# Layer 1's end rebuilt: gathers that centre by themselves, the bonus added in PSUM, the last state product on VectorE, the channel mix by halves in the same section

## What is computed

```python
def step(s, rkvw):                       # s: 8x8 state of each of 32 heads
    r_t, k_t, v_t, w_t = rkvw
    a = k_t[:, :, :, None] * v_t[:, :, None, :]
    out = jnp.einsum('bhk,bhkd->bhd', r_t, u * a + s)
    return (a + w_t[:, :, :, None] * s, out)
_, outs = jax.lax.scan(step, s0, xs)
a4 = outs as (b, l, H, 8)                # per head: subtract the mean, divide by the deviation
m = jnp.mean(a4, axis=-1, keepdims=True)
var = jnp.mean((a4 - m) ** 2, axis=-1, keepdims=True)
att = ((a4 - m) * jax.lax.rsqrt(var + EPS)).reshape(b, l, E) * gn_w + gn_b
x = x + att * g @ Wo.T
xn2 = _ln(x, ln2_w, ln2_b)
sx2 = _token_shift(xn2, state[:, i0])    # row before minus row
xk = xn2 + sx2 * ffn_maa_k
xr = xn2 + sx2 * ffn_maa_r
rr = jax.nn.sigmoid(xr @ ffn_Wr.T)
kk = jnp.square(jax.nn.relu(xk @ ffn_Wk.T))
x = x + rr * (kk @ ffn_Wv.T)
```

## Time and profile before

| | |
|---|---|
| median of the runs | 1258.51 us |
| the profiled execution | 1257.39 us, span 1255.70 |
| mean granted clock of TensorE | 0.981 |
| PE, DVE, ACT, POOL busy | 91%, 65%, 51%, 54% |
| state loop, layer 1's end | about 816 to 880 us, 880 to 942 us |

### The profile page before, as it was taken

One profiled execution on the slowest core, in us unless ns is written; L12 is line 12 of the kernel. 1 busy time (PEld: TensorE's weight loads), 2 busy tenths in 40 slices (PEclk: granted clock), 3 DMA queues, 4 the chain that ended last, 5 costly groups with the idle time before them and its releaser, 6 DMA issues. The chain is left out here.

```text
span 1255.7 us, 20660 instructions
## 1 busy us (share of the span) xinstructions
PE 1142.1 (91%) x7388; PEld 889.8 (71%) x7388; DVE 822.2 (65%) x2013; ACT 642.1 (51%) x1428; POOL 683.9 (54%) x742
## 2 busy tenths in 40 slices
PE   5999999999999999999998967987578999999996
PEld 4788888887978788888887852443355676667674
DVE  6776666676656766667666545598557655666774
ACT  3655654566545555565566111510325655777764
POOL 3656664666645656556575312386005655566874
PEclk9999999999999999999999988999889999999999
DMA  6210220121102210221020200000001100000000
GB/s 213 67 44 26 68 67 16 53 68 62 56 18 67 68 44 25 68 68 51 18 68 17 84 17 0 1 1 0 1 0 61 35 2 1 2 1 2 10 10 18
DMA packets 35111, 47.06 MB, mean 37 GB/s; under 512 B 3865, under 2 KB 22082, under 8 KB 35010
## 3 DMA queue, kind: packets, MB, share of 16 engines
q1 hardware_dynamic: 34640, 44.83, 11.3%
q10 hardware_dynamic: 370, 0.91, 0.2%
HBM read 44.69 MB, written 1.05 MB: 36 GB/s over the span
## 5 line engine op out<-in xcount | busy, mean ns | idle before, releaser
L444 POOL TENSOR_TENSOR a_prob<-a_prob,a_inv_total 128x512 f32<-128x512 f32 x128 | 144.2, 1126 | 208.2 <-DVE a_inv_total L732 208.2
L1967 POOL TENSOR_TENSOR scores<-scores,neg_max 128x512 f32<-128x512 f32 x144 | 147.5, 1040 | 77.4 <-DVE neg_max L1835 77.2
L637 ACT ACTIVATE a_prob<-psum,a_neg_max 128x257 f32<-128x257 f32 x256 | 119.0, 472 | 94.3 <-DVE a_neg_max L729 93.4
L1758 ACT ACTIVATE prob_T<-psum 128x512 f32<-128x512 f32 x192 | 113.1, 600 | 35.5 <-PE psum L1679 34.1
L1679 PE MATMUL psum<-ident,scores 128*128 128x128 f32 x768 | 117.8, 279 | 1.5 <-POOL scores L1967 1.5
L1679 PEld LDWEIGHTS psum<-ident,scores 128*128 128x128 f32 x768 | 85.7, 141 | 36.8 <-issue 16.3
L736 DVE TENSOR_TENSOR a_probT_lo<-psum,a_probT_hi 128x512 fp32r<-128x512 f32 x128 | 88.0, 687 | 32.5 <-ACT a_probT_hi L641 32.0
L1835 DVE CUSTOM_DVE_ANT_0 scores<-psum,ctx_rows 128x256 f32<-128x256 f32 x256 | 93.5, 420 | 18.7 <-PE psum L1666 9.3
L566 PE MATMUL psum<-ident,a_prob 128*128 128x128 f32 x512 | 77.8, 274 | 24.0 <-DVE a_probT_lo L736 21.7
L566 PEld LDWEIGHTS psum<-ident,a_prob 128*128 128x128 f32 x512 | 60.0, 140 | 44.5 <-issue 20.9
L641 ACT ACTIVATE a_probT_hi<-psum 128x512 fp32r<-128x512 f32 x128 | 76.7, 599 | 22.2 <-PE psum L566 22.2
(11 more groups left out here) (347 smaller groups left out, 3340.7 us busy)
## 6 DMA issues: line engine op xcount, KB each, us to landing
wk_raw<-in_L_xattn_wk SPq DMA_DIRECT2D x16, 512.0 KB, 6.3
wq_raw<-in_L_xattn_wq SPq DMA_DIRECT2D x16, 512.0 KB, 5.6
wv_raw<-in_L_xattn_wv SPq DMA_DIRECT2D x16, 512.0 KB, 3.7
wo_raw<-in_L_xattn_wo SPq DMA_DIRECT2D x16, 512.0 KB, 3.9
ctx_rows<-in_ctx SPq DMA_DIRECT2D x3, 512.0 KB, 4.1
x_rows<-in_x SPq DMA_DIRECT2D x2, 512.0 KB, 9.7
ctx_rows<-in_mask_Bx1xSxS_ff SPq DMA_DIRECT2D x1, 1024.0 KB, 5.5
out_dram<-x_rows SPq DMA_DIRECT2D x4, 256.0 KB, 2.1
```

The lines of the kernel that those rows point to most:

```text
L444: pool.tensor_tensor(prob[:, m % 4, :, 0:S], prob[:, m % 4, :, 0:S], rtot[:, m % 4, :].unsqueeze(2).to_broadcast([P, 2, S]), ALU.mult)
L637: act.activation(prob[:, m % 4, q, 0:S + 1], s_bank(g)[:, q, 0:S + 1], ACT.Exp, bias=negm[:, m % 4, q:q + 1], accum_out=tot[:, m % 4, q:q ...
L1758: act.activation(pT[:, i % PT, :], t_bank(i), ACT.Exp, scale=1.0 if on_scalar(i) else -1.0).then_inc(exp_ok, 1)
L1967: pool.tensor_tensor(sc[:, i % SC, :, :], sc[:, i % SC, :, :], m[:, i % SC, :].unsqueeze(2).to_broadcast([P, 2, S]), ALU.subtract).then_in ...
```

## The change

The gather matrices hold -1/8 for every row of the head and 7/8 for the row itself, so that what they sum has the head's mean subtracted; they are now made on DVE. A matrix `centre` (identity less 1/8 over the head) adds the bonus to the same banks, one matmul for each piece. Mean, centring and the adds on DVE are gone. The second half of the last product z is made by DVE. PE's order at the end of the loop is another. The banks of the following steps are swapped (variances and Wo in 0 to 3, layer norm in 4 to 7). The layer norm runs its statistics and normalise for both halves behind the adds. The channel mix stands in the same section, reuses the section's buffers and takes the tokens by halves; the sigmoid's scaling is folded into its last two operations.

```diff
 # PE
+                def gather_outputs(g, cs):
+                    for c in cs:
+                        pe.wait_ge(z_ok, NC * g + c + 1)
+                        for n in (2 * c, 2 * c + 1):
+                            mm = pe.matmul(ps[:, 4 + n, :], gather[:, g, :], z[g % 2][:, c, half(n)], start=g == 0, stop=g == S1 - 1)
+                            if g == S1 - 1:
+                                mm.then_inc(g_full, 1)
...
+                def gather_bonus(n):
...
+                    pe.matmul(ps[:, 4 + n, :], centre[:, :], att[:, n // 2, half(n)], start=False, stop=False)
+
+                for e in range(2, S1):
+                    spread_values(e, 0)
+                    if e == S1 - 1:
+                        gather_outputs(e - LATE, range(NC))
+                    spread_values(e, 1)
...
+                    if e < S1 - 1:
+                        gather_outputs(e - LATE, range(NC))
+                    if e >= 5:
+                        gather_bonus(e - 5)
+                gather_bonus(3)
+                gather_outputs(S1 - 2, range(NC))
+                gather_outputs(S1 - 1, range(NC))
...
 # DVE
+                dve.scalar_tensor_tensor(centre[:, :], same[:, :], -1.0 / S1, chip.ident[:, :], ALU.mult, ALU.add).then_inc(centre_ok, 1)
                 for e in range(S1):
-                    dve.tensor_copy(gather[:, e, e:P:S1], same[:, e:P:S1]).then_inc(gather_ok, 1)
+                    dve.tensor_scalar(gather[:, e, :], same[:, :], -1.0 / S1, None, ALU.mult).then_inc(gather_low, 1)
+                for e in range(S1):
+                    dve.wait_ge(gather_low, e + 1)
+                    dve.tensor_scalar(gather[:, e, e:P:S1], same[:, e:P:S1], 1.0 - 1.0 / S1, None, ALU.mult).then_inc(gather_ok, 1)
...
+                        if (e, c) == LAST:
+
+                            dve.wait_ge(g_full, S1 - 2)
+                            dve.wait_ge(st_ok, S1 * NC)
+                            dve.wait_ge(z_ok, S1 * NC - 1)
+                            dve.tensor_tensor(z[e % 2][:, c, :], rT[:, c, :], flat(state[:, e % 2, c, :, :]), ALU.mult).then_inc(z_ok, 1)
...
-                for i, n in enumerate(SEQ):
-                    dve.wait_ge(g_full, S1 + i)
-                    dve.tensor_tensor(att[:, n // 2, half(n)], att[:, n // 2, half(n)], ps[:, 4 + n, :], ALU.add).then_inc(att_ok, 1)
-                    if i >= 2:
-                        centre(i - 2)
...
-                    ln.after_rows(dve, q)
+                    if q % 2:
+                        ln.statistics(dve, q // 2)
+                for h in range(2):
+                    ln.normalise(dve, h)
+                channel_mix_vector(dve)
 # ACT
+                for n in range(4):
+                    act.wait_ge(g_full, S1 + n)
+                    act.activation(sq[:, n // 2, half(n)], ps[:, 4 + n, :], ACT.Square).then_inc(sq_ok, 1)
 # the channel mix: DVE, then PE
+            for h in range(2):
+                dve.wait_ge(ln.turned_out, 2 * h + 2)
+                for c in range(NC):
+                    dve.tensor_tensor(sx2[:, c, two(h), :], xe[:, c, two(h), 0:S], xe[:, c, two(h), 1:R1], ALU.subtract).then_inc(cm_shifted, 1)
+                mix(xk, 'L1_xattn_ffn_maa_k', h)
+                mix(xr, 'L1_xattn_ffn_maa_r', h)
+                if h:
+                    for c in range(NC):
+                        square(c, 0)
+            for c in range(NC):
+                square(c, 1)
...
+            for h in range(2):
+
+                pe.wait_ge(cm_mixed, 4 * h + 2)
+                for c in range(NC):
+                    n = 2 * c + h
+                    for k in range(NC):
+                        mm = pe.matmul(ps[:, n, :], w['ffn_Wk'][:, k, c * P:(c + 1) * P], flat(xk[:, k, two(h), :]), start=k == 0, stop=k == NC - 1)
+                    mm.then_inc(k_full, 1)
+                pe.wait_ge(cm_mixed, 4 * h + 4)
+                pe.wait_ge(ln.turned_out, 4)
+                for t in range(4 * h, 4 * h + 4):
...
```

More of the change, by code:

```diff
@@ L928, in stage_rwkv @@
         kv_of = lambda c: ps[:, 2 * c:2 * c + 2, :].rearrange("p h n -> p (h n)")
+        cm_first, cm_shifted, cm_mixed, k_full, relu_ok, kk_ok, r_full, tanh_ok, o2_full, t_ok = (
+            chip.semaphore(f"cm_{n}") for n in ("first", "shifted", "mixed", "k_full", "relu_ok", "kk_ok", "r_full", "tanh_ok", "v_full", "t_ok"))
+        sx2, xr = wT, first
+        xk = rT[:, :, :].rearrange("p c (b s) -> p c b s", s=S)
+        kk = state[:, 0].rearrange("p c b s -> p c (b s)")
+        tanh_r = state[:, 1].rearrange("p c b s -> p (c b s)").rearrange("p (t n) -> p t n", n=D)
@@ new lines, in stage_rwkv, with channel_mix_vector, mix, square @@
+        gated_v = scaled[:, 0].rearrange("p c n -> p (c n)").rearrange("p (t n) -> p t n", n=D)
+        two = lambda q: slice(2 * q, 2 * q + 2)
+        def channel_mix_vector(dve):
+            def mix(dst, name, h):
+                for c in range(NC):
+                    dve.wait_ge(cm_shifted, 2 * h + c + 1)
+                    dve.scalar_tensor_tensor(dst[:, c, two(h), :], sx2[:, c, two(h), :], chip.vec(name, c), xe[:, c, two(h), 1:R1], ALU.mult, ALU.add).then_inc(cm_mixed, 1)
+            def square(c, h):
+                dve.wait_ge(relu_ok, 2 * h + c + 1)
+                n = 2 * c + h
+                dve.scalar_tensor_tensor(kk[:, c, half(n)], ps[:, n, :], 0.0, kk[:, c, half(n)], ALU.max, ALU.mult).then_inc(kk_ok, 1)
+            dve.wait_ge(cm_first, 1)
+            for h in range(2):
[9 more added lines that the diff above has]
+                square(c, 1)
+            for q in range(4):
+                dve.wait_ge(o2_full, q + 1)
+                dve.wait_ge(tanh_ok, q + 1)
+                dve.scalar_tensor_tensor(gated_v[:, two(q), :], tanh_r[:, two(q), :], 1.0, ps[:, 2 * (q % 2) + q // 2, :].rearrange("p (j n) -> p j n", j=2), ALU.add, ALU.mult).then_inc(t_ok, 1)
+                dve.wait_ge(t_ok, q + 1)
+                dve.scalar_tensor_tensor(chip.x[:, two(q), :], gated_v[:, two(q), :], 0.5, chip.x[:, two(q), :], ALU.mult, ALU.add)
@@ new lines, in channel_mix_scalar @@
+        def channel_mix_scalar(act):
+            for h in range(2):
+                for c in range(NC):
+                    n = 2 * c + h
+                    act.wait_ge(k_full, 2 * h + c + 1)
+                    act.activation(kk[:, c, half(n)], ps[:, n, :], ACT.Relu).then_inc(relu_ok, 1)
+                for q in (2 * h, 2 * h + 1):
+                    act.wait_ge(r_full, q + 1)
+                    act.activation(tanh_r[:, two(q), :], ps[:, 4 + q, :].rearrange("p (j n) -> p j n", j=2), ACT.Tanh, scale=0.5).then_inc(tanh_ok, 1)
@@ L1029, in _ @@
+                    if e >= 5:
[4 more added lines that the diff above has]
+                for n in range(4):
+                    pe.wait_ge(sq_ok, n + 1)
+                    pe.matmul(ps[:, n, :], same[:, :], sq[:, n // 2, half(n)], start=True, stop=True).then_inc(var_full, 1)
                 for t in range(NT):
                     if t % 4 == 0:
-                        pe.wait_ge(gated, 2 + 2 * (t // 4))
@@ L1098, in _, with norm @@
                             dve.scalar_tensor_tensor(gT[:, c, half(n)], tanh_of(n), 1.0, ps[:, bank_of(('pg', n)), :], ALU.add, ALU.mult).then_inc(dve_free, 1)
[L1100 removed]
+                def norm(i):
                     n = SEQ[i]
[L1102 to L1112 removed]
+                    dve.wait_ge(rstd_ok, i + 1)
+                    dve.scalar_tensor_tensor(att[:, n // 2, half(n)], ps[:, 4 + n, :], chip.vec('L1_xattn_gn_w', n // 2), sq[:, n // 2, half(n)], ALU.mult, ALU.mult).then_inc(gn_ok, 1)
                 def gate(i):
@@ L1118, in gate @@
                                              ALU.add, ALU.mult).then_inc(gated, 1)
-                for i, n in enumerate(SEQ):
-                    c = n // 2
-                    dve.wait_ge(rstd_ok, i + 1)
-                    dve.scalar_tensor_tensor(att[:, c, half(n)], att[:, c, half(n)], chip.vec('L1_xattn_gn_w', c), sq[:, c, half(n)], ALU.mult, ALU.mult).then_inc(gn_ok, 1)
+                for i in range(4):
+                    norm(i)
                     if i:
```

160 lines of the change are left out of this document (45 added, 115 removed).

## The result

The changed kernel takes 1246.26 us (median of 4 runs, 1244.27 to 1246.60) against 1257.99 (4 runs) before; the ratio is 0.9903, 95% interval 0.9886 to 0.9920. The forecast was 1245.9. The four executions of each kernel are apart by 2.1 to 2.3 us, so a difference of less than about 1 us between two medians says nothing. In the profiled executions the span went from 1255.7 to 1244.0, and layers 2 and 3, from PE's first transposes to the end, take 312.1 in both: all of the difference lies ahead of them.

What follows compares the result with a forecast made beforehand. The prediction took the stretch as one chain through all engines with nothing beside it, except the DVE-bound state loop. 2.8 + 4.2 + 5.6 = 12.6 us off 1258.51 gave 1245.9, range 1242.5 to 1249.5.

Steps and rivals of the forecast that it cites:

- Part 1: Last gathers at the state loop's end: new PE order and VectorE's half product end them 2.8 us earlier.
- The fall at the last gathers: PE's drop to half clock there before the change; runs without it would miss 1.7 us of gain, giving 1247.6.
- Part 2: Bonus, mean and centring behind the last gathers: ACT squares PSUM directly, 4.2 us gained.
- Parts 3 and 4: Layer norm order and channel mix by halves behind Wo: PE's first channel mix product 5.6 us earlier.
- a case for which the prediction gave 6.2: Layer norm's eight transposes at full clock instead of half: channel mix starts 6.2 us earlier; 5.6 was taken.
- the order of the normalises: Layer norm with both normalises behind the adds: second half gains 1.35 us, first half loses 2.3.
- barrier and copy: Ahead of the channel mix's shift: 0.5 us, counted inside the 5.5 us of earlier start.
- The stream of 22.7: PE's channel mix work: same amount, 22.7 us without running dry, first four records at half clock.
- rival B: Kinder clock at the channel mix: 2.0 us less there, 0.7 less for transposes, 1243.2 us; chance 0.14.
- C: Last spread late at the last gathers through half clock: 1.5 to 2.5 us lost, 1247.4 to 1248.4; chance 0.16.
- D: Channel mix halves wait for one another on DVE: gain only 8.85 us, 1249.7 us; chance 0.05.
- E: PE at half clock through the channel mix: 19.2 us more, 1265 us; chance 0.02.

Runs made afterwards that it cites:

- part1_alone: Kernel before with only the new order of the last gathers and the last half product z on VectorE, no bonus matmuls: 1254.11 us.
- z_on_pool: Changed kernel with the second half of the last product z back on POOL: 1246.61 us.
- busy_before: Kernel before with matmuls of no use in PE's holes ahead of Wo, between the halves' transposes and ahead of the channel mix: 1255.67 us.
- norm_between: Changed kernel with the first half's normalise between the last two adds, as before the change: 1247.88 us.
- wait_both: Changed kernel, but PE's first channel mix product waits for the mixes of both halves: 1251.85 us.
- bonus_early: Changed kernel with the four bonus matmuls in pairs in two earlier turns of the state loop, none behind the last spread: 1246.73 us.
- mix_first: Changed kernel with first half's shift and mix ahead of second half's normalise, and second half's transposes behind the first product: 1247.31 us.
- busy: Changed kernel with matmuls of no use in PE's holes ahead of Wo, ahead of the layer norm's transposes and ahead of the channel mix: 1243.37 us.
- busy_bonus: The busy kernel with bonus_early's edit, the bonus matmuls in pairs in two earlier turns of the state loop: 1241.16 us.

## Why the prediction was right

The parts that the prediction named are the ones that gave the time, and each total came out within 0.4 us. How the totals are made up was in part wrong, and the last digits of 1245.9 are luck.

- **Part 1, 2.8**: measured 2.83 (9.57 to 6.74), with PE as the bound and its records where the sum put them. But it was two terms: 4.1 for the order and VectorE's help together, 1.7 of it the fall of the clock, less 1.3 for the bonus (part1_alone); and in the changed kernel the help does nothing (z_on_pool). The fall at the last gathers stood in both profiles with the old order of the kernel before (before and busy_before), and in none of the others. Whether the other executions of before have it stays open.
- **Part 2, 4.2**: measured 4.11, from 10.70 to 6.59.
- **Parts 3 and 4, 5.6**: measured 5.85 (23.74 to 17.89). The first transposes ran at full clock, a case for which the prediction gave 6.2, so 0.35 of that did not come. The split was wrong: the order of the normalises was booked at 1.35, taken from the second half, though PE waits only for the first. It is worth 0.5 (norm_between), and the halves 3.9 (wait_both). The 1.4 left agrees with 0.5 for barrier and copy and 0.87 for the transposes at full clock, neither of which was run by itself.
- **The stream of 22.7, unchanged**: 0.36 shorter, since the clock rose earlier in it (1.51 lost in its first eight records, 1.86 before). That is the cause of rival B, at a fifth of the 2.0 that B gave the stream. C, D and E did not come about.
- **The sum**: 2.83 + 4.11 + 5.85 + 0.36 = 13.15 in the profile against 12.6.
- **What the sum did not have**: 1.47 came off again ahead of the change, so that the spans differ by 11.7. The profiled execution of the changed kernel reaches the first state 1.47 later. It was 1.86 later already at the last add of layer 0 (741.55 against 739.69), in code that is the same. There the same matmuls stood at half clock in one and at full in the other. Before, then after (columns as in the window above):

```profile
728.40:731.80 3.40, 3.40 (x31) 3.40 (x31) 0.00 (x0) 0.00 (x0) 0.00 (x0) 1.00 0.00 0
```
```profile
728.40:731.80 3.40, 3.40 (x16) 3.40 (x17) 0.00 (x0) 0.00 (x0) 0.00 (x0) 0.51 0.00 0
```

Over the fourteen profiles the first state starts anywhere from 808.6 to 811.8, and in z_on_pool, which has the same code up to there as the changed kernel, at 809.35. So this is the execution and not the change. The Trainium skill, "TensorE: Matmul & The Clock Gate", Part 1, says that the number of slow matmuls varies from run to run. The trace agrees: 16 records in one execution and 31 in the other, in the same 3.40 us.

The medians moved by 11.7 too, though the stretches of the change sum to 13.2 in the profiles. Whether the missing 1.5 is the chance of a few runs, or the changed kernel more often meets a fall further on (as three of its variants and busy_before do in layers 2 and 3), stays open. The four runs of the changed kernel point at the clock: 1244.27 and 1245.98 had a mean granted clock of 0.985 and 0.984, 1246.53 and 1246.60 one of 0.979.

The forecast hit within 0.4 us in part by luck. It took 12.6 from 1258.51, the median of three runs; with the fourth that median is 1257.99, 0.5 lower, and the gain was 11.7, 0.9 smaller.

## What to carry to other kernels

In a stretch that is one chain, price it piece by piece from the timeline and add the pieces; here each of the four totals held to 0.4 us. A wrong split can hide in such a total: ask for each term what bounds it before and after, and run the parts alone. When a cut makes PE wait in other places, look at the clock before believing that the cut did nothing: of bonus_early's 0.85 us, 0.65 was lost to it in one profile, and with PE kept at work the whole 0.85 stood there. The clock is not always the reason, though: mix_first showed no gain in the median with PE kept at work either. And cut the profile into stretches before comparing two versions: the same code differed by 2 to 3 us between executions, more than most of the edits were worth.

## What the runs showed that was not expected

- Matmuls of no use in the holes gave 2.9 us on the changed kernel and 2.1 on the one before, by the medians. PE's granted clock was 1.00 from 881.5 to 924.0 in busy.
- Layers 2 and 3 took 312.1 to 312.3 us in ten of the fourteen profiles and 314.3 to 314.5 in four, with the same code. In busy, one of the four, the clock fell twice at their start:

```profile
927.00:931.00 4.00, 3.63 (x18) 2.75 (x19) 3.93 (x20) 2.17 (x4) 3.37 (x11) 0.65 0.57 170
...
948.00:954.00 6.00, 6.00 (x31) 5.00 (x28) 2.66 (x13) 2.07 (x5) 5.41 (x6) 0.72 0.00 0
```

  Ahead of the second fall PE had worked 2.96 of 4.00 us (943.94 to 947.94). In busy_bonus the same two stretches, 0.8 earlier, stood at full clock:

```profile
926.20:930.20 4.00, 3.03 (x19) 2.37 (x20) 3.90 (x20) 2.06 (x4) 3.36 (x11) 1.00 0.51 164
947.20:953.20 6.00, 6.00 (x39) 4.99 (x38) 3.73 (x17) 1.88 (x5) 5.01 (x7) 1.00 0.01 3
```

- In the changed kernel POOL's power on 128x4 took 1.24 us beside the normalise of VectorE (900.35) and 1.02 for the first half, where VectorE ran adds (896.90).
